# Rotary halves by a VectorE shuffle, and the later query and key products moved into the attention rounds

## The reference, cut to what matters

```python
q = (xq @ Wq).reshape(b, n, HEADS, DH).transpose(0, 2, 1, 3) * DH ** (-0.5)
k = (ctx @ Wk).reshape(b, j, HEADS, DH).transpose(0, 2, 1, 3)
# apply_rope, on the first 32 of 64 channels
t1 = t1 * cos(freqs) + concatenate([-t1[..., 16:], t1[..., :16]]) * sin(freqs)
sim = einsum('bhid,bhjd->bhij', q, k)
out = (softmax(sim) @ v) @ Wo + bo
```

## Time and profile before

| | |
|---|---|
| median of 3 runs | 4449.32 us (4441.46 to 4451.9) |
| profiled execution, its own time | 4439.93 us |
| profiled execution, its span | 4437.0 us |
| mean granted TensorE clock | 0.982 of full |
| instructions | 71100 |

### The profile page before, as it was taken

How to read it: one execution, slowest core, us unless ns; L and a number is a source line. 1 busy time by engine, 2 the same in 40 slices (tenths; PEclk the granted TensorE clock), 3 DMA queues, 4 the chain that set the end, 5 groups by cost and what they waited for, 6 DMA issues and landing times. The chain is left out here.

```text
span 4437.0 us, 71100 instructions
## 1 busy us (share of the span) xinstructions
PE 4059.2 (91%) x24156; PEld 2465.6 (56%) x24156; DVE 2674.6 (60%) x7163; ACT 1998.3 (45%) x5804; POOL 861.7 (19%) x972
## 2 busy tenths in 40 slices
PE   7988899999999998889989988999999999988899
PEld 4644456555556555555646444565555566555555
DVE  4687576666666645654446785766666666456544
ACT  2731445455445434663227313554554454346632
POOL 2146222112221200000020462222112212000000
PEclk9999999999999999999999999999999999999999
DMA  2000000000000010010010000000000000100000
GB/s 88 5 16 1 16 7 17 22 17 22 16 22 1 25 55 20 14 51 9 4 59 17 1 1 22 1 16 22 17 22 16 22 2 24 55 20 37 27 9 10
DMA packets 15849, 91.87 MB, mean 21 GB/s; under 512 B 2176, under 2 KB 8064, under 8 KB 12032
## 3 DMA queue, kind: packets, MB, share of 16 engines
q1 hardware_dynamic: 15488, 87.27, 5.4%
HBM read 86.22 MB, written 1.05 MB: 20 GB/s over the span
## 5 line engine op out<-in xcount | busy, mean ns | idle before, releaser
L564 PE MATMUL ps_O<-wide,V 128*64 128x256 f32 (+4 forms) x5152 | 597.1, 394 | 1.9 <-ACT wide L588 1.8
L633 ACT ACTIVATE EX<-NB,neg 128x154 f32<-128x154 f32 (+3 forms) x640 | 350.2, 551 | 399.8 <-DVE neg L658 399.7
L606 POOL COPY RX<-recips 128x256 f32<-128x256 f32 (+2 forms) x356 | 156.8, 440 | 1818.0 <-DVE recips L673 1754.4
L684 DVE TENSOR_TENSOR QT<-ps_O,RS 128x512 f32<-128x512 f32 x212 | 146.6, 692 | 444.8 <-PE ps_O L564 442.7
L588 ACT ACTIVATE wide<-ps_P 128x512 f32<-128x512 f32 (+2 forms) x648 | 367.6, 569 | 60.6 <-PE ps_P L546 60.5
L546 PE MATMUL ps_P<-consts,EX 128*128 128x128 f32 (+1 forms) x2148 | 316.4, 281 | 77.5 <-ACT wide L588 40.2
L399 POOL TENSOR_TENSOR small<-small 128x4 f32<-128x4 f32 x112 | 113.5, 1014 | 1407.3 <-DVE small L384 895.9
L515 PE MATMUL ps_S<-KT,QT 64*128 64x154 f32 (+7 forms) x1936 | 363.2, 458 | 25.7 <-issue 14.6
L564 PEld LDWEIGHTS ps_O<-wide,V 128*64 128x64 f32 (+4 forms) x5152 | 267.5, 128 | 195.6 <-issue 112.6
L515 PE MATMUL ps_OUT<-KT,QT 64*128 64x154 f32 (+5 forms) x968 | 331.5, 436 | 0.4 <-ACT EX L633 0.4
L590 DVE COPY wide<-ps_P 128x512 f32<-128x512 f32 (+4 forms) x404 | 259.4, 643 | 115.6 <-PE ps_P L546 115.0
(11 more groups left out here) (353 smaller groups left out, 8211.7 us busy)
## 6 DMA issues: line engine op xcount, KB each, us to landing
weights<-in_w_dram SPq DMA_DIRECT2D x10, 1664.0 KB, 6.8
weights<-in_w_dram SPq DMA_DIRECT2D x2, 6148.0 KB, 17.0
weights<-in_w5next_dram SPq DMA_DIRECT2D x6, 1664.0 KB, 6.9
weights<-in_w_dram SPq DMA_DIRECT2D x2, 4200.0 KB, 12.3
weights<-in_reltab_dram SPq DMA_DIRECT2D x2, 4096.0 KB, 13.4
weights<-in_w_dram SPq DMA_DIRECT2D x8, 640.0 KB, 3.9
weights<-in_w_dram SPq DMA_DIRECT2D x5, 832.0 KB, 4.3
weights<-in_w_dram SPq DMA_DIRECT2D x2, 2050.0 KB, 7.8
```

The lines of the kernel that those rows point to most:

```text
L564: ins = pe.matmul(O1[self.slot * j:self.slot * (j + 1), q0 * P:(q0 + self.nq) * P], self.value(c * self.hpc + j, kc), self.probs(rd, j)[:, ...
L606: pool.tensor_copy(RX[:, q0 * P:(q0 + self.nq) * P].rearrange("p (n s) -> p n s", s=self.slot), of.unsqueeze(2).broadcast_to([P, self.nq * ...
L633: ins = act.activation(ex[:, a * N:(a + 1) * N], src, ACT.Exp, bias=neg[:, at:at + 1], scale=-1.0 if self.added else 1.0, accum_out=sums[: ...
L684: dve.tensor_tensor(self.out_chunk(c), O1[:, :], RS[:, c % 2, :], ALU.mult).then_inc(r.av_sb, 1)
```

## The change: what it does

- The swapped product is no longer made. VectorE instead shuffles partitions of the one product inside each group of 32, lane m from lane (m + 16) mod 32, from PSUM into `part`; it multiplies the bank by cos into KT or QT, and `part` by sin in place, for q with a table `sinq` that holds 0.125 sin and is made once at the start. In self-attention the multiply by sin is GpSimd's for all but the first two products. GpSimd's add is kept. The swapped weights are still loaded.
- The order is k0, q0, k1, q1 and so on, and chunk c waits for 2c + 2 rotated products. The front holds products 0 to 3 and the value products. Self-attention makes products 4, 5, 6 and 7 at the ends of iterations 1, 2, 3 and 4; cross-attention makes 4 and 5 at the end of iteration 0 and 6 and 7 at the end of iteration 1. They take banks of the transposes' ring, in turn.
- The other lane's X is transposed at the end of iteration 2, in a bank of the same ring, and copied by ScalarE at the start of iteration 3. `fill` and `fill2` are gone from these steps.
- In the iterations that follow a late product, ScalarE empties a turned bank ahead of the exponential of the same k, not behind it.
- VectorE does the head parts of the next step in other places: the sums of squares after two products, the scaling after iteration 1. In cross-attention the tail of the step before is now ahead of the products.
- The other steps with attention keep their order.

```diff
+        HALVES = [(m + 16) % 32 for m in range(32)]
+        def rope(dve, r, bank, dst, part, scale, wait, j, sin):
+            n = dst.shape[-1]
+            if wait:
+                dve.wait_ge(*wait)
+            dve.stream_shuffle(part, bank, HALVES).then_inc(r.evac_dve, 1)
+            if scale is None:
+                dve.tensor_tensor(dst, bank, K("cos")[:, 0:n], ALU.mult).then_inc(r.evac_dve, 1)
+            else:
+                dve.scalar_tensor_tensor(dst, bank, scale, K("cos")[:, 0:n], ALU.mult, ALU.mult).then_inc(r.evac_dve, 1)
+            if sin is not None:
+                dve.wait_ge(r.evac_dve, 2 * j + 1)
+                dve.tensor_tensor(part, part, sin, ALU.mult).then_inc(r.sum_step, 1)
...
+                    for j in self.late.get(i, ()):
+                        if self.late_at[j] >= nb:
+                            self.evacuated(pe, r, self.late_at[j] - nb)
+                        late(pe, j)
...
+                    turn_first = 1 <= i <= self.rounds and i - 1 in self.late
                     for k in range(4):
+                        if turn_first:
+                            if k == 0 and i >= 2 and (i - 1) % self.rpc == 0:
+                                self.turn_recips(act, r, (i - 1) // self.rpc - 1)
+                            self.turn(act, r, "A", i - 1, k, free)
...
-                self.order = [("k", c) for c in range(4)] + [("q", c) for c in range(4)]
+                self.order = [(m, c) for c in range(4) for m in "kq"]
-                                     queries=lambda c: (self.r.rotated, 4 + c + 1))
+                                     queries=lambda c: (self.r.rotated, 2 * c + 2),
+                                     late={0: [4, 5], 1: [6, 7], 2: ["X"]} if cross else {1: [4], 2: [5, "X"], 3: [6], 4: [7]})
...
+                self.front = Table(ropes + values if cross else ropes[0:2] + values + ropes[2:4])
...
+            def rotate(self, pool, j):
+                r, d, part = self.r, self.dest(j), self.part(j)
+                pool.wait_ge(r.evac_dve, 2 * j + 2)
+                if not self.cross and j >= 2:
+                    pool.tensor_tensor(part, part, self.sines(j), ALU.mult).then_inc(r.sum_step, 1)
+                pool.wait_ge(r.sum_step, j + 1)
+                pool.tensor_tensor(d, d, part, ALU.add).then_inc(r.rotated, 1)
...
+                parts = self.parts()
+                parts[0][0](dve, parts[0][1])
+                evacuate(dve, r, self.front, "D", 0, 2)
+                parts[1][0](dve, parts[1][1])
+                evacuate(dve, r, self.front, "D", 2)
```

More of the change, by code:

```diff
@@ L181, in ch, with parts @@
         return self.chain
+    def parts(self):
+        return [(self.prev.tail, n) for n in range(self.prev.tail_parts)] + \
+            [(self.nxt.head, n) for n in range(self.nxt.head_parts)]
     def beside(self, dve, *which):
@@ L209, in build @@
         consts = sb("consts", [P, nconsts])
+        sinq = sb("sinq", [P, SEQ])
         lora_bias = sb("lora_bias", [P, 4])
@@ L636, in act, with dve @@
                             ins.then_inc(r.exped, 1)
-                        if k == 0 and i >= 2 and (i - 1) % self.rpc == 0:
+                        if k == 0 and i >= 2 and (i - 1) % self.rpc == 0 and not turn_first:
                             self.turn_recips(act, r, (i - 1) // self.rpc - 1)
-                        if 1 <= i <= self.rounds:
+                        if 1 <= i <= self.rounds and not turn_first:
                             self.turn(act, r, "A", i - 1, k, free)
-            def dve(self, dve, r, free=None, beside=None):
+            def dve(self, dve, r, free=None, beside=None, late=None):
                 for i in range(self.steps):
+                    for j in self.late.get(i - 1, ()):
+                        if j != "X":
+                            late(dve, j)
                     for k in range(4):
@@ L1500, in __init__ @@
+                ropes = [([self.product(j)], P, self.size(j), "D", "rope", self.dest(j), self.turning(j)) for j in range(4)]
                 values = [([(src[:, c * kc:(c + 1) * kc], w("wv"))], kc, SEQ, "A", "copy",
                            v_rows(kc, 8, 64, 64, c), None) for c in range(nch)]
-                self.tab = Table([row for j in range(8) for row in self.rotary(j)])
-                self.values = Table(values, self.tab)
-            def dest(self, m, c):
-                return QT[:, c, :] if m == "q" else KT[:, c, 0:self.NK]
@@ new lines, in product, with sines, turning @@
+            def product(self, j):
+                m, c = self.order[j]
+                return self.w("w" + m)[:, c * P:(c + 1) * P], self.L.XT[:, :] if m == "q" else self.src[:, :]
+            def sines(self, j):
+                return (sinq if self.order[j][0] == "q" else K("sin"))[:, 0:self.size(j)]
+            def turning(self, j):
+                return (self.part(j), 0.125 if self.order[j][0] == "q" else None, self.before(j), j,
+                        self.sines(j) if self.cross or j < 2 else None)
@@ new lines, in late_pe, with late_dve @@
+            def late_pe(self, pe, j):
+                if j == "X":
+                    self.nxt.pe_head(pe, self.att.late_bank(j))
+                    return
+                if j == 4:
+                    pe.wait_ge(self.r.evac_dve, self.front.d)
+                    pe.wait_ge(self.r.evac_act, self.front.a)
+                pe.matmul(self.att.late_bank(j)[:, 0:self.size(j)], *self.product(j), start=True, stop=True
+                          ).then_inc(self.r.proj, 1)
+            def late_dve(self, dve, j):
+                dve.wait_ge(self.r.proj, self.front.j1 + j - 3)
+                rope(dve, self.r, self.att.late_bank(j)[:, 0:self.size(j)], self.dest(j), *self.turning(j))
@@ L1521, in pool @@
                 self.fresh(pool)
-                for j in range(8):
-                    m, c = self.order[j]
-                    d = self.dest(m, c)
-                    pool.wait_ge(r.evac_dve, 2 * j + 2)
-                    pool.tensor_tensor(d, d, self.part[j % 4][:, 0:SEQ if m == "q" else self.NK], ALU.add
-                                       ).then_inc(r.rotated, 1)
-                self.att.pool(pool, r)
+                self.rotate(pool, 0)
+                self.rotate(pool, 1)
+                self.prev.pool_tail(pool)
```

129 lines of the change are left out of this document (67 added, 62 removed).

## The result

The changed kernel takes 4287.64 us (4 runs, 4285.66 to 4290.27), the kernel before on the same chip 4450.17 (4441.46 to 4451.9): ratio 0.9639, 95% interval 0.9622 to 0.9656. That is 162 us less; 149 were predicted, and the forecast of 4300 is 12 us high. Between the two profiled executions it is 153 us (4439.93 to 4286.59), and 152 in their spans (4437.0 to 4284.9): the 9.4 us by which the median of the kernel before lay above its profiled execution had been added to the forecast, and after the change the median lies 1 us above.

A forecast was written before the change was run, and what follows sets the result against it. TensorE was taken to bind the kernel. Gains of 6.0 us a self step and 3.3 a cross step, times 16, gave 149 us off 4439.9, so 4291; with 9.4 for the median, 4300 us, range 4258 to 4392.

The forecast's parts named there:

- Rival (a): Whole kernel: TensorE binds everywhere and all 182 us of removed work are gained, 4267 us; chance 10%.
- (b): Start of each step: more latency at some ten handovers and one more add in VectorE's way, 88 us, 4388; chance 22%.
- (d): The shuffle costs far more than 0.6 us; at 2 us each the kernel is 53 us slower, 4502; chance 6%.
- (e): Between the rounds: late products and X hold the ring of banks, leaving 43 us of gain, 4406; chance 7%.
- The same work in other places: Late products and the turning of X: moved to later iterations, they were taken to be the same work as before.
- The shuffle's price: VectorE's shuffle from PSUM: 0.60 us for 512 columns, 0.26 for 154, at most 1.2; some nine a pair on the path.
- lane list: A load possibly needed beside each shuffle: between nothing and 0.28 us, taken as 0.1.
- The self step: Self-attention, worked through from the first product: gain 6.3 us less 0.3 for lane lists, 6.0, so 65.4 us a step.
- The stop that the prediction saw: VectorE's two-operand instructions standing until GpSimd's add ends: about 0.65 us in a self step, 1.8 in a cross step.
- The cross step: Cross-attention, worked through from its start: gain 3.7 us less 0.4 for lane lists, 3.3 of 4.5, so 39.5 us a step.
- k1 and q1 with three passes each run to 8.8: Cross front: VectorE finishes these products at 8.8 us, with one stop behind GpSimd's power; second scores go at 10.3.
- Rival (c): Lane 0 crosses: a thinner start lets TensorE's granted clock fall in more places, 14 to 27 us, 4320; chance 15%.

The follow-up runs named there:

- e_twice: The changed kernel with every shuffle made twice, the first time into a scratch tile: 4391.18 us, ratio 0.9885 to the kernel before.
- v3: The changed kernel with self-attention's sums of squares and GpSimd's power for them moved ahead of the first product's shuffle: 4285.09 us, ratio 0.9656.
- second run: The changed kernel executed once more with nothing changed: 4286.84 us, the same span of 4284.9.
- z_shift: The changed kernel with three matmuls that nobody reads added once in each pass, in lane 1's last feed-forward part: 4285.71 us, ratio 0.9655.
- e_frame: The kernel before, in its order, with only the swapped products replaced by shuffle, cos and sin on VectorE: 4557.18 us, ratio 1.0255.
- e_nolate: The changed kernel with products 4 to 7 made in the front as well, with their three passes: 4630.65 us, ratio 1.0431.
- e_sindve: The changed kernel with all of self-attention's multiplies by sin on VectorE, GpSimd keeping only its add: 4330.45 us, ratio 0.9753.
- v1: The changed kernel with self k1 and q1 ahead of the last two value products, and sums of squares and the cross tail later: 4275.79 us, ratio 0.9624.
- v2: The changed kernel with self-attention's sums of squares and GpSimd's power for them moved behind the maxima of iteration 0: 4298.91 us, ratio 0.9686.
- e_turnlast: The changed kernel with ScalarE's order as before, exponential first and the turned bank behind it: 4350.15 us, ratio 0.9797.
- v4: The changed kernel without the small 128x4 multiply, its 1/128 put into the sums of squares, and self k1 and q1 mostly earlier: 4251.68 us, ratio 0.9583.

## Why the prediction was right

**What is removed.** 512 records fewer, as counted, and TensorE stayed the engine that binds; the forecast's mechanism held: a pass lost 74.3 us of TensorE's busy time and opened no new standing. Rival (a) didn't come, since TensorE still stands 2.9 us of each cross step (38.30 less 35.44), nor did (b), (d) and (e). (In (e) five waits of 0.7 us are 3.5, not the 3.3 of its sum, which makes it 4409.) "The same work in other places" was a little too cheap: a late product takes TensorE 1.03 us from its start to the next scores' (868.85 to 869.88), the other three 0.96 to 1.06, where one of the front takes 0.86; that is 0.7 us a self step.

**The shuffle's price** was taken as 0.60 us for 512 columns and measured 0.62; for 154 columns 0.23. The lane list was taken as 0.1 and is 0.01: the 0.7 us a pair counted for it are not spent. Of the shuffles a pair it had nine on the path; by e_twice there are some seven. By the estimate from the Trainium skill (VectorE: DVE Perf Modes, the perf-mode tier table) a shuffle was 0.6 for 512, and the trace agrees.

**The self step.** First scores at 7.02 (predicted 6.9), first maximum at 9.03 (9.5), second scores at 9.8 (10.3), iteration 2 at 15.6 (15.8); the step 65.5 (65.4). Here every time was right to 0.5 us, the step's with some luck: the start gained 9.5 us where 9.3 were counted, and the rounds gave back 3.6 where 3.0 and 0.3 of lane lists were; the lane lists cost nothing, and the late products' longer time stands in their place. The stop that the prediction saw, on the multiply by sin, is there but small (0.83 in place of 0.68, 858.41). The long one was on an instruction that it had not listed, the 128x4 multiply. Sums of squares make GpSimd wait too: its add began 0.3 us late at 859.67. The Trainium skill (VectorE: DVE Perf Modes, what auto-detection actually checks) has an operation with one source take two ports when source and destination are in SBUF and their outermost dimensions are both even or equal; the 1.27 us beside an add, against 0.17 without one (v3), agree.

**The cross step** is the term that was mis-sized: 38.3, where 39.5 was predicted, a gain of 4.5 instead of 3.3. The first scores are right (5.08, predicted 5.0), the second come at 8.9, not 10.3, and the third, from 15.7 on, are over by about 17.3 instead of 18.2. The step "k1 and q1 with three passes each run to 8.8" failed: VectorE was done with the squares by 5.0 instead of 5.6 and with these products by 7.5, without the stop behind the power (925.17 above). The crosses of lane 1 gained 5.1 each with the feed-forward part behind them, since there the fall of the clock of the earlier trace rows is gone too.

**The sum.** A sublayer went from 246.2 to 224.7 us, 10.75 for a pair where 9.3 was predicted; times 16 that is 172. The span gained 152, 20 less. The first self step of each pass is one reason: its front gains 2.4 us and not 7.4 (13.5 from first product to first scores, against 16.0). ScalarE's squares need an X that is ready only at 565.5, the copies of V are queued behind them, and the value products, now in the front, wait 4.36 us for banks. The prediction missed that wait. Not all of it is lost, for behind the first scores this step gains 3 us more than the others, and from its first product to the next step's it takes 72.7 us against 76.8 before, 2 us less gain than in the others; that is 4 us in all. The larger part lies where the change does nothing: what stands ahead of the first pass ends 1.9 us later, what lies between the first scores of the last cross and the next pass's first product is 7.2 us longer, and what is behind the second pass 4.3 (734.9 against 730.6). The clock granted between the passes is 0.96, and it was 0.97. Errors of both signs, +23 and -20, met in a sum that looks better than its parts.

**Rival (c)** had the clock fall more often in the crosses. Rather, most of the falls in the crosses of before are gone (a pass at 1.00), and the unchanged steps have some more of them. The second run and z_shift show that such a fall comes and goes without any change to its steps; what decides over it stays open, and so does whether the 13 us there belong to the change or to chance. The mechanism of (c) is real all the same, in the kernels where TensorE stands longer: the same matmuls of a pass took 15.5 us more in e_twice, 32.5 in e_frame, 31.4 in e_nolate and 13.6 in e_sindve, each at a lower granted clock (0.98, 0.91, 0.92, 0.98).

**What the gain is made of.** It is the busy time of the products that are gone, but it isn't to be had by leaving them out alone: e_frame saves all of them and loses 114 us. Between e_frame and the changed kernel lie 270 us, in a pass three parts of standing to one of lower clock. Without ScalarE's new order the changed kernel is 62 us slower, without GpSimd's multiplies 43. These two are not shares of the 270, since each was left out of the whole by itself, and no run makes only the first half of the products in the front without the other parts. Nor was the other way round tried, the new order with the swapped products kept.

## What to carry to other kernels

Taking work from the engine that binds pays only if the engines that take it over are not what the next stage waits for: swap the work and move it in one step, and look at what the shared ring, buffers and ports then wait for. When VectorE and GpSimd work side by side, look in the timeline for small instructions with long records: a 128x4 multiply cost 1.1 to 1.3 us, moving it moved the wait or opened another (v1, v2, v3), and removing it together with an earlier k1 and q1 gave more than any move. A wait of the engine that binds can be paid twice: look whether the same matmuls take longer behind it, as they do in e_frame and e_sindve and hardly in e_turnlast. Differences below some 5 us of a kernel like this one are to be read in the steps, not in the total.

## What the runs showed of the hardware beyond the expected

- A shuffle over lanes from PSUM costs what a copy does: 0.72 us on record against 0.69 for 128x512.
- The stop between VectorE and GpSimd works in both directions: GpSimd's add of 1.27 us takes 1.40 when it starts under a sum of squares (923.37; 853.37 in v4), and 1.42 in v2 (1096.29).
- GpSimd's power over 128x4 (1.02 us) doesn't stop a multiply of VectorE with two operands in SBUF: 0.30 us at 925.17, against 0.31 at 921.10 with GpSimd idle.
- One fall of the granted clock in an unchanged stretch costs 2.7 us (82.59 against 79.85), and it comes and goes between two runs of one kernel. The steps ahead of the first pass are the same in the changed kernel, e_turnlast and v3, and took 556.9, 561.5 and 555.0 us.
